# Query bias as rows in four column groups, two shared chunks two and one tiles earlier, identity products at tile 3

## The chip, the cores and the metric

The kernel runs on one core of one Trainium2 chip. The metric is the device time of one execution in microseconds (us), median over several runs; a profiled execution is one run more, with a trace of every instruction.

## The reference, cut to what matters

The program is one adaptive-LayerNorm block over X of 2 x 1024 tokens of 512 features. Six modulation vectors for each of the two batches come from `silu(c) @ wmod`. The first half is an attention of a special kind, the second a mixture of experts:

```python
h = _layernorm(x) * (1 + ca) + sa
# attention: A is one vector of 512 for each batch
Xn = _layernorm(h, gamma, beta)
Q, K, V = split(Xn @ W_in + b_in)
K, V = rotary(K), rotary(V)
A = 0.5 * sum_over_tokens(K / |K| * V / |V|) + 0.5
Y = (A * Q) @ W_out + b_out + h
x = x + ga * Y
h = _layernorm(x) * (1 + cb) + sb
# experts: a shared one of width 704 and the best 2 of 8 of width 352
x = x + gb * (shared(h) + routed(h))
```

Since Xn is `normed * gamma + beta`, the query has the constant part `beta @ W_q + b_q`, a vector of 512: the query bias.

## The kernel before, in words

Tokens go in 16 tiles of 128 rows. TensorE (PE) does the large products in three fp32r passes, high times high, high times low, low times high (`product3`, L1560 to L1562); ScalarE writes the high part of an operand (`tokens_hi`, `tokens2_hi`) and VectorE subtracts it from the original for the low part (`tokens_lo`, `tokens2_lo`). Each engine has its own instruction list, written out by hand, and works it off in order; semaphores (`wait_ge`, `then_inc`) tie them. There is no planner.

First pass, 16 tiles: K products, the transposes of the next tile, V products (`kv_matmul`, `transposes`), and the rotated, weighted sums of the tile before (`weighted_sums`). Among them stand small steps through one PSUM bank, named in the list `MISC`; `SLOT_A` says behind which tile's K products, `SLOT_B` behind which tile's V products. Each waits (`misc_read`) until the one before it in `MISC` has been read, by ScalarE or, for those in `BY_VECTOR`, by VectorE. `mod` (tile 5) makes the modulation rows in four groups of 32 columns; `q0` to `q3` turn the query weights; `qbias` (tile 6) makes `beta @ W_q` as a column: four output columns, four products of one column for each.

Then W_q, scaled by A, is multiplied by W_out (`m_matmul`, `h_matmul`), 179 to 188 us, so that the second rows need one product for each tile.

Second rows, a loop over 16 tiles t, 188 to 277 us. TensorE: `y_matmul(t)`, 13 products of 512 columns; at t = 6, 10, 14 `logit_parts` for four finished tiles and a tile later `gate_logits`; `transposes2(t - 2)`; and at the tiles of `Y_CHUNKS` a chunk of the shared expert's gate and up products for tiles 0 to 3 (`shared_gate_up(0, (m,))`, 24 products of 512 columns). Chunk 0 waits for `t2_lo` of four tiles, which VectorE raises in `tokens2_lo`. VectorE, in iteration t: `second_rows(t)` with the statistics (L1183, L989 to L991), `residual_part(t + 1)` (L1173), `tokens2_lo(t - 2)` (L1202), for t < 2 two blocks of the second batch's matrix (L1147, L1152), `ffn_rows(t)` (L1195, L1197), and for chunks `s_lo_of` and `s_mul_of`. ScalarE: `tokens2_hi(t - 2)` (L796, L797), `x_normed(t + 2)`, and for chunks `s_silu_of` and a tile later `s_hi_of`. `y_matmul(t)` waits for `x2_ready` of tile t - 2, `transposes2(t - 2)` for `h2_ready` of that tile. SyncE (SP) stores rows and loads the next X tile once for each t.

Behind the loop come the rest of the shared expert, the routing and, from about 400 us, a loop over experts, all with TensorE without gaps.

The activation buffer of the shared expert is `gbuf[n % 3]`, three buffers that lie in `bc_s`, `bc_c` and `bc_ga`; `bc_s` is still read by `ffn_rows` for the first batch.

Of the kernel before, what the change touches and what calls it, by code (L numbers as in the profile page):

```python
# [51 lines left out]
EW = 2 * DC * H + NR * D  # L52


Y_CHUNKS = {8: 0, 10: 1, 12: 2, 14: 3}


MISC = ["sin_a", "cos_a", "s1", "c1", "sin_b", "cos_b", "q0", "q1", "q2", "q3", "mod", "qbias", "a0", "a1"]
BY_VECTOR = ("c1", "mod", "qbias", "a0", "a1")
SLOT_A = {1: ["s1"], 2: ["sin_b"], 3: ["q0"], 4: ["q2"]}  # L60
SLOT_B = {0: ["sin_a", "cos_a"], 1: ["c1"], 2: ["cos_b"], 3: ["q1"], 4: ["q3"], 5: ["mod"], 6: ["qbias"], 9: ["a0"]}


def build(nc, X, W_in, b_in, W_out, b_out, gamma, beta, gate_w, w_gate, w_up, w_down,
# [10 lines left out]
    with ctx:  # L75
# [171 lines left out]
        rawkv = [slots[:, 2 + i, :].rearrange("p (k n) -> p k n", k=DC) for i in range(2)]  # L247
        cos, sin = slots[:, 0, 0:S], slots[:, 0, S:2 * S]
        MOD_SLOT = (2, 3, 1, 0)

        bank = [ctx.enter_context(nc.psum_tensor(f"bank{i}", [P, GN], F32)) for i in range(8)]
        T_BANKS, K_BANKS, V_BANKS, W_BANK, MISC_BANK = (0, 1), (2, 4), (3, 5), 6, 7
# [385 lines left out]
        def _(act):  # L638
# [31 lines left out]
            def tokens_hi(t):  # L670

                act.wait_ge(t_mm, t + 1)
                if t == 2 * GT:
                    act.wait_ge(misc_mm, MISC.index("mod") + 1)
                nc.scalar.activation(tokens(t, 0), chunked(bank[T_BANKS[t % 2]][:, :]), ACT.Copy).then_inc(t_hi, 1)

            def k_row(t):
# [19 lines left out]
            def read_misc(name):  # L697

                n = MISC.index(name)
                src = bank[W_BANK if name == "cos_a" else MISC_BANK][:, :]  # L700
                act.wait_ge(misc_mm, n + 1)
                if name == "s1":
                    last = nc.scalar.activation(bc_s[:, 1, :], src, ACT.Copy)
                elif name[0] == "q":
                    last = nc.scalar.activation(wqT[:, int(name[1]), :], src, ACT.Copy)
                else:
                    half = slice(0, GT) if name[-1] == "a" else slice(GT, NB)
                    src = src.rearrange("p (t f) -> p t f", t=GT)
                    if name[0] == "s":
                        last = nc.scalar.activation(cs[:, half, 0, :], src, ACT.Copy, scale=2.0)  # L710
                    else:
                        last = nc.scalar.activation(cs[:, half, 1, :], src, ACT.Identity, bias=ones[:, 0:1], scale=-2.0)
                last.then_inc(misc_read, 1)
# [92 lines left out]
            def s_silu_of(g, m):  # L806
                n = NS * g + m
                r = SM[m]
                act.wait_ge(s_gu_mm, n + 1)
                if n == 0:  # L810
                    act.wait_ge(h2_ready, NB)
                if n >= 3:
                    act.wait_ge(s_lo, n - 2)
                nc.scalar.activation(gbuf[n % 3][0:r, :], bank[gate_banks(g, m)[0]][0:r, :], ACT.Silu).then_inc(s_silu, 1)

            def s_hi_of(g, m):
                n = NS * g + m
                r = SM[m]
                act.wait_ge(s_mul, n + 1)
                if g:  # L820
                    act.wait_ge(s_down_mm, GT * g)
                nc.scalar.activation(gtS[0:r, m, 0, :], gbuf[n % 3][0:r, :], ACT.Copy).then_inc(s_hi, 1)

            for i in range(DC):
                m_block_hi(0, i)
# [136 lines left out]
        def _(dve):  # L962
# [242 lines left out]
            def s_mul_of(g, m):  # L1205
                n = NS * g + m
                r = SM[m]
                dve.wait_ge(s_silu, n + 1)
                up = bank[gate_banks(g, m)[0]][r:P, :] if r == P // 2 else bank[gate_banks(g, m)[1]][0:r, :]
                dve.tensor_tensor(gbuf[n % 3][0:r, :], gbuf[n % 3][0:r, :], up, ALU.mult)\  # L1210
                    .then_inc(s_mul, 1)

            def s_lo_of(g, m):
                n = NS * g + m
                r = SM[m]
                dve.wait_ge(s_hi, n + 1)
                to = gtS[:, m, 1, :] if r == P else gtS[r:P, m, 0, :]
                dve.tensor_tensor(to, gbuf[n % 3][0:r, :], gtS[0:r, m, 0, :].bitcast(F32), ALU.subtract)\
                    .then_inc(s_lo, 1)

            dve.wait_ge(ga_in, 16)
# [335 lines left out]
        def _(pe):  # L1557
# [62 lines left out]
            def misc(name):  # L1620

                n = MISC.index(name)
                to = bank[W_BANK if name == "cos_a" else MISC_BANK]
                if n < 2:
                    pe.wait_ge(bias_ready, 2)
                else:
                    pe.wait_ge(misc_read, n)
                if name in ("s1", "c1"):
                    last = spread_row((MISC_BANK), 1, 0 if name == "s1" else 1)
                elif name[0:3] in ("sin", "cos"):  # L1630
                    src = cos if name[0] == "s" else sin
                    pe.wait_ge(sincos if name[0] == "s" else sinsq, 1)
                    for j in range(GT):
                        at = (j + (GT if name[-1] == "b" else 0)) * P
                        last = nc.tensor.transpose(to[:, j * P:(j + 1) * P], src[:, at:at + P], ident[:, :])
                elif name == "qbias":
                    for m in range(DC):
                        for k in range(DC):
                            last = nc.tensor.matmul(to[:, m:m + 1], q_columns(k, m), gb_col[:, 1, k:k + 1],
                                                    start=k == 0, stop=k == DC - 1)  # L1640
                elif name[0] == "q":
                    pe.wait_ge(wq_in, 32)
                    for k in range(DC):
                        last = nc.tensor.transpose(to[:, k * P:(k + 1) * P], q_columns(k, int(name[1])), ident[:, :])
                elif name == "mod":
                    for k in range(DC):
                        pe.wait_ge(mod_in[k], 16)
                    for k in range(DC):
                        for v in range(4):
                            last = nc.tensor.matmul(to[Q4 * v:Q4 * v + B, :], scT[:, k, :],  # L1650
                                                    slots[:, MOD_SLOT[k], v * D:(v + 1) * D],
                                                    start=k == 0, stop=k == DC - 1)
                else:
                    b = int(name[1])
                    pe.wait_ge(arow_ready, b + 1)
                    pe.wait_ge(consts, 5)
                    for two in range(2):
                        nc.tensor.matmul(to[:, 0:2], arow[:, b, two:ROT:2], asel[:, 2 * two:2 * two + 2],
                                         start=two == 0, stop=two == 1)
                    for half in range(2):  # L1660
                        last = nc.tensor.matmul(to[:, 2 + half:3 + half], arow[:, b, half * P:(half + 1) * P],
                                                asel[:, 4:5], start=True, stop=True)
                last.then_inc(misc_mm, 1)

            def q_columns(k, m):

                return rawq[:, k, m:ROT:2] if m < 2 else rawq[:, k, m * P:(m + 1) * P]
# [68 lines left out]
            def shared_gate_up(g, chunks=range(NS)):  # L1736
                for m in chunks:
                    n, r = NS * g + m, SM[m]
                    if m == 0:
                        pe.wait_ge(t2_lo, GT * (g + 1))  # L1740
                        if g == 0:
                            pe.wait_ge(sg_lo, DC)
                    if n in range(1, DC + 1) or n == DC + 1:
                        pe.wait_ge(s_mul, n - (n == DC + 1))
                    elif n:
                        pe.wait_ge(s_mul, n - 1)
# [102 lines left out]
            def y_matmul(t):  # L1849
# [9 lines left out]
                if t == 0:  # L1859
                    pe.wait_ge(bh_ready, 1)  # L1860
                nc.tensor.matmul(to, pair1[:, b:b + 1].to_broadcast([P, P]), bh[:, :], start=False, stop=True)\
                    .then_inc(y_mm, 1)

            def transposes2(t):
                pe.wait_ge(h2_ready, t + 1)
                if t >= 2:
                    pe.wait_ge(t2_lo, t - 1)
                for k in range(DC):
                    last = nc.tensor.transpose(bank[T2_BANKS[t % 2]][:, k * P:(k + 1) * P],  # L1869
                                               hx[:, t % GT, k * P:(k + 1) * P], ident[:, :])  # L1870
                last.then_inc(t2_mm, 1)
# [16 lines left out]
                nc.tensor.transpose(bank[LG_BANK][:, g * P:(g + 1) * P], turned, ident[:, :]).then_inc(lg_mm, 1)  # L1888

            for t in range(NT):  # L1890
                y_matmul(t)
                if t >= 6 and t % GT == 2:
                    logit_parts((t - 6) // GT)
                if t >= 7 and t % GT == 3:
                    gate_logits((t - 7) // GT)
                if t >= 2:
                    transposes2(t - 2)
                if t in Y_CHUNKS:
                    shared_gate_up(0, (Y_CHUNKS[t],))
# [70 lines left out]
```

## Time and profile before

| | us |
|---|---|
| median of 3 runs | 719.1 |
| lowest and highest | 715.85, 719.9 |
| the profiled execution | 717.99 |
| its span, first to last instruction | 716.2 |
| TensorE products busy | 682.1 |
| VectorE, ScalarE, GpSimd busy | 469.6, 258.0, 169.4 |
| mean granted clock of TensorE | 0.982 of 2.4 GHz |

The span is shorter than the execution by what lies around it. Busy time of TensorE is that of its products, which overlap: a 512-column product lasts 0.39 us in the records and the next starts 0.23 us behind it, so starts, not durations, are what is subtracted here. A float32 product that isn't fp32r is two records. A clock of 0.50 is 1.2 GHz.

### The profile page before, as it was taken

How to read it: one execution, taken by the hardware profiler on the slowest of the kernel's cores; microseconds unless marked ns; L12 is line 12 of the kernel's file. 1: busy time of each engine (PE TensorE's matmuls, PEld its weight loads, DVE VectorE, ACT ScalarE, POOL GpSimd, SP SyncE). 2: the span in 40 equal slices, each digit the busy share in tenths (PEclk: the TensorE clock that was granted, in tenths of full speed). 3: DMA queues.
4: the chain of work that ended last, by engine and by line, in shares of the span. 5: the costliest groups of instructions: out<-in, count | busy, mean ns of one | idle time of the engine just before them, and what ended most of it. 6: DMA issues, size and time to landing. Idle time of an engine off the chain costs nothing.

```text
span 716.2 us, 10569 instructions
## 1 busy us (share of the span) xinstructions
PE 682.1 (95%) x3796; PEld 562.6 (79%) x3796; DVE 469.6 (66%) x967; ACT 258.0 (36%) x478; POOL 169.4 (24%) x221
## 2 busy tenths in 40 slices
PE   5899999999979999999999999999999999999992
PEld 1477677777857887887887887989898998989891
DVE  1987769836899886467767835665574847556451
ACT  1555344535344342412013024435362534436130
POOL 1232223310012110000000032334435353540403
PEclk9799999999999999999999999999999999999997
DMA  8923131104135624230320533657665575852505
GB/s 275 361 84 104 38 83 30 41 4 162 59 133 177 213 89 135 86 106 13 103 96 1 165 107 118 192 120 191 103 198 73 187 131 148 193 97 59 67 0 67
DMA packets 44219, 82.52 MB, mean 115 GB/s; under 512 B 7529, under 2 KB 15721, under 8 KB 43634
## 3 DMA queue, kind: packets, MB, share of 16 engines
q1 hardware_dynamic: 35730, 62.06, 26.8%
q0 software_dynamic: 8448, 19.93, 14.6%
q8 instruction: 24, 0.39, 0.2%
q14 instruction: 17, 0.14, 0.1%
HBM read 59.93 MB, written 23.22 MB: 116 GB/s over the span
## 4 chain that ended last, share of the span: by engine, by line
PE 63%; DVE 8%; issue 2%; ACT 1%; POOL 1%; POOLq 0%; DVEq 0%
PE bank L1560 19%; PE bank L1562 19%; PE bank L1561 19%; PE bank L1811 2%; PE bank L1791 1%; DVE rows L1183 1%; DVE u L1173 1%; DVE m L1147 1%; DVE st L989 1%; DVE hx L1195 1%; DVE mw L1152 1%; POOL out_rows L613 1%; PE bank L1869 1%; PE bank L1770 0%; PE bank L1882 0%
## 5 line engine op out<-in xcount | busy, mean ns | idle before, releaser
L1560 PE MATMUL bank<-ht,ew 128*128 128x288 f32 (+1 forms) x384 | 114.6, 299 | 0.2 <-DVE ht L1458 0.2
L1561 PE MATMUL bank<-ht,ew 128*128 128x288 f32 (+1 forms) x384 | 113.1, 294 | 0.0
L1562 PE MATMUL bank<-ht,ew 128*128 128x288 f32 (+1 forms) x384 | 112.8, 294 | 0.0
L613 POOL DMA_INDIRECT out_rows<-y,si x40 | 61.9, 1547 | 110.7 <-DVE y L1489 100.0
L1560 PE MATMUL bank<-xt,sgu 128*128 128x512 f32 x176 | 69.5, 395 | 0.4 <-DVE rows L1183 0.4
L1560 PEld LDWEIGHTS bank<-ht,ew 128*128 128x128 f32 (+1 forms) x384 | 68.7, 179 | 1.3 <-issue 0.6
L1561 PEld LDWEIGHTS bank<-ht,ew 128*128 128x128 f32 (+1 forms) x384 | 69.0, 180 | 0.3
L1562 PEld LDWEIGHTS bank<-ht,ew 128*128 128x128 f32 (+1 forms) x384 | 68.7, 179 | 0.0
L1561 PE MATMUL bank<-xt,sgu 128*128 128x512 f32 x176 | 68.7, 390 | 0.0
L1562 PE MATMUL bank<-xt,sgu 128*128 128x512 f32 x176 | 68.6, 390 | 0.0
L1560 PE MATMUL bank<-wkv,xt 128*128 128x512 f32 x128 | 55.2, 431 | 2.8 <-DVE xt L1018 2.8
L1448 DVE TENSOR_TENSOR ew<-ewst,ew 128x1408 fp32r<-128x1408 f32 (+2 forms) x32 | 40.5, 1289 | 18.9 <-ACT ew L872 11.3
L1562 PE MATMUL bank<-wkv,xt 128*128 128x512 f32 x128 | 52.0, 406 | 0.0
L1561 PE MATMUL bank<-wkv,xt 128*128 128x512 f32 x128 | 51.8, 404 | 0.0
L1489 DVE TENSOR_TENSOR y<-bank,gsel 128x512 f32<-128x512 f32 (+1 forms) x40 | 27.5, 688 | 35.2 <-PE bank L1562 35.2
L602 POOL DMA_INDIRECT picked<-h_d,gi x40 | 44.3, 1107 | 24.1 <-issue 9.8
L1560 PE MATMUL bank<-ew,gtR 128*128 128x512 f32 (+3 forms) x120 | 48.4, 403 | 0.0
L1561 PE MATMUL bank<-ew,gtR 128*128 128x512 f32 (+3 forms) x120 | 47.4, 395 | 0.0
L1562 PE MATMUL bank<-ew,gtR 128*128 128x512 f32 (+3 forms) x120 | 47.3, 394 | 0.0
L594 POOL COPY gi<-gidx 128x5 int32 (+1 forms) x8 | 1.9, 240 | 164.8 <-DVEq L1437 127.1
L544 POOL TENSOR_TENSOR rs<-ve,nhalf 128x1 f32<-128x1 f32 x16 | 15.4, 960 | 101.7 <-DVE ve L991 101.7
L1560 PEld LDWEIGHTS bank<-xt,sgu 128*128 128x128 f32 x176 | 33.1, 188 | 7.4 <-issue 0.8
(302 smaller groups left out, 1512.1 us busy)
## 6 DMA issues: line engine op xcount, KB each, us to landing
xring<-in_L_attn_X SPq DMA_DIRECT2D x32, 256.0 KB, 2.8
ewst<-in_L_ffn_w_gate SPq DMA_DIRECT2D x8, 704.0 KB, 5.3
ewst<-in_L_ffn_w_up SPq DMA_DIRECT2D x8, 704.0 KB, 4.3
slots<-in_L_wmod SPq DMA_DIRECT2D x4, 1024.0 KB, 6.1
x_d<-rows SPq DMA_DIRECT2D x16, 256.0 KB, 2.0
h_d<-hx SPq DMA_DIRECT2D x16, 256.0 KB, 2.0
xrow<-x_d SPq DMA_DIRECT2D x16, 256.0 KB, 2.8
out_rows<-xrow SPq DMA_DIRECT2D x16, 256.0 KB, 2.2
```

The source lines that it names most:

```text
L544: pool.tensor_tensor(rs[:, 2, t:t + 1], ve[:, 2, t:t + 1], nhalf[:, 0:1], ALU.pow).then_inc(rs3_ready, 1)
L602: pool.indirect_dma_start(out=picked[par][:, j, :], out_offset=None, in_=h2_d, in_offset=bass.IndirectOffsetOnAxis(ap=gi[:, par, j:j + 1], ...
L613: pool.indirect_dma_start(out=out, out_offset=bass.IndirectOffsetOnAxis(ap=si[0:CR[j], par, j:j + 1], axis=0), in_=y[0:CR[j], j, :], in_of ...
L989: link(dve.bn_stats(st6[:, :], row))
L1147: dve.scalar_tensor_tensor(m32[:, i, :], bank[M_BANKS[b][i]][:, :], gb_col[:, 0, i:i + 1], bc_ga[:, b, :], ALU.mult, ALU.mult).then_inc(m3 ...
L1152: dve.tensor_tensor(mw[:, b, 1, i, :], m32[:, i, :], mw[:, b, 0, i, :].bitcast(F32), ALU.subtract)\
L1448: last = dve.tensor_tensor(ew[par][0:r, 1, a:z], ewst[0:r, slot, at:at + z - a], ew[par][0:r, 0, a:z].bitcast(F32), ALU.subtract)
L1489: dve.tensor_tensor(y[0:r, j, :], bank[DOWN_BANKS[(par + j) % 2]][0:r, :], gsel[0:r, j, :], ALU.mult)\
L1560: nc.tensor.matmul(dst, a[0], b[0], start=first, stop=False)
L1561: nc.tensor.matmul(dst, a[0], b[1], start=False, stop=False)
L1562: return nc.tensor.matmul(dst, a[1], b[0], start=False, stop=last)
L1811: last = nc.tensor.transpose(bank[RT_BANKS[(par + s) % 2]][:, i * P:(i + 1) * P], picked[par][:, j, k * P:(k + 1) * P], ident[:, :])
```

## The change

1. A new small step `qrow` behind the K products of tile 6: four float32 products of 512 columns, one for each block of 128 input features, each into its own group of 32 output columns. ScalarE copies the result to a free slot, and `qbias` behind the V products of the same tile becomes four one-column products that add the four groups and turn the row. ScalarE's high part of tile 8 waits for `qbias` instead of `mod`, because it overwrites that slot.
2. `Y_CHUNKS`: chunk 0 stands behind tile 6 instead of 8, chunk 1 behind 9 instead of 10. The three buffers are taken in another order, so that the first chunk needs none that tiles below 8 still read; the waits of ScalarE follow.
3. `busy`: eight float32 products of a 128 x 128 identity with itself ahead of `y_matmul(3)` and eight behind it, whose result nobody reads.

```diff
-Y_CHUNKS = {8: 0, 10: 1, 12: 2, 14: 3}
+Y_CHUNKS = {6: 0, 9: 1, 12: 2, 14: 3}
-MISC = [..., "q3", "mod", "qbias", "a0", "a1"]
+MISC = [..., "q3", "mod", "qrow", "qbias", "a0", "a1"]
-SLOT_A = {1: ["s1"], 2: ["sin_b"], 3: ["q0"], 4: ["q2"]}
+SLOT_A = {1: ["s1"], 2: ["sin_b"], 3: ["q0"], 4: ["q2"], 6: ["qrow"]}
+        qrow = slots[:, 3, 0:D]
...
                 if t == 2 * GT:
-                    act.wait_ge(misc_mm, MISC.index("mod") + 1)
+                    act.wait_ge(misc_mm, MISC.index("qbias") + 1)
...
+                elif name == "qrow":
+                    last = nc.scalar.activation(qrow, src, ACT.Copy)
...
                 if n == 0:
+                    act.wait_ge(m32_ready, B * DC)
+                if n == 1:
                     act.wait_ge(h2_ready, NB)
...
-                nc.scalar.activation(gbuf[n % 3][0:r, :], ...Silu).then_inc(s_silu, 1)
+                nc.scalar.activation(gbuf[(n + 2) % 3][0:r, :], ...Silu).then_inc(s_silu, 1)
...
                 act.wait_ge(s_mul, n + 1)
+                if n == 0:
+                    act.wait_ge(y_mm, NB)
...
                 elif name == "qbias":
                     for m in range(DC):
-                        for k in range(DC):
-                            last = nc.tensor.matmul(to[:, m:m + 1], q_columns(k, m), gb_col[:, 1, k:k + 1],
-                                                    start=k == 0, stop=k == DC - 1)
+                        columns = qrow[:, m:ROT:2] if m < 2 else qrow[:, m * P:(m + 1) * P]
+                        last = nc.tensor.matmul(to[:, m:m + 1], columns, rowsel[:, 0:1], start=True, stop=True)
+                elif name == "qrow":
+                    pe.wait_ge(wq_in, 32)
+                    for k in range(DC):
+                        last = nc.tensor.matmul(quarter(to, k), gb_col[:, 1, k:k + 1].to_broadcast([P, Q4]), rawq[:, k, :],
+                                                start=True, stop=True)
...
                         if g == 0:
                             pe.wait_ge(sg_lo, DC)
+                            pe.wait_ge(m32_ready, B * DC)
...
+            def busy(to, times):
+                for _ in range(times):
+                    nc.tensor.matmul(to[:, 0:P], ident[:, :], ident[:, :], start=True, stop=True)
...
             for t in range(NT):
+                if t == 3:
+                    busy(bank[T2_BANKS[1]], 8)
                 y_matmul(t)
+                if t == 3:
+                    busy(bank[T2_BANKS[1]], 8)
```

VectorE's two operations on the chunks (`s_mul_of`, `s_lo_of`) take the buffers in the new order too.

## Rows read from the trace of the kernel before

**Rows 1.** The page: TensorE's busy time, and the clock in forty slices.

```profile
PE 682.1 (95%) x3796; PEld 562.6 (79%) x3796; DVE 469.6 (66%) x967; ACT 258.0 (36%) x478; POOL 169.4 (24%) x221
...
PEclk9799999999999999999999999999999999999997
```

**Rows 2.** The waits of TensorE: for whom, us in total, times, longest.

```profile
PE bank L1560 <- DVE rows L1183: 2.8, 3, 1.2
```

**Rows 3.** Order of time, TensorE, tiles 5 to 7: start, us, instruction.

```profile
77.45 0.40 PE L1617 MATMUL bank<-bv,pairs 128*128 128x512 f32 x1
77.78 3.62 PE L1650 MATMUL bank<-slots,scT 128*2 128x512 f32 x32
81.22 0.39 PE L1678 MATMUL bank<-prod,wtok 128*32 128x256 f32 x2
...
81.76 0.50 PE L1560 MATMUL bank<-wkv,xt 128*128 128x512 f32 x1
...
84.62 0.40 PE L1617 MATMUL bank<-bk,pairs 128*128 128x512 f32 x1
...
85.22 0.48 PE L1560 MATMUL bank<-wkv,xt 128*128 128x512 f32 x1
...
88.29 3.72 PE L1639 MATMUL bank<-gb_col,rawq 128*128 128x1 f32 x32
91.94 0.41 PE L1678 MATMUL bank<-prod,wtok 128*32 128x256 f32 x2
...
92.51 0.50 PE L1560 MATMUL bank<-wkv,xt 128*128 128x512 f32 x1
...
96.96 0.40 PE L1617 MATMUL bank<-bk,pairs 128*128 128x512 f32 x1
```

**Rows 4.** Stretches: length, PE, PEld, DVE, ACT, POOL busy, PE clock, DMA.

```profile
93.50:96.90 3.40, 3.40 (x9) 2.65 (x9) 1.26 (x5) 0.00 (x0) 0.74 (x2) 0.50 0.29 101
...
206.20:209.60 3.40, 3.40 (x9) 2.64 (x10) 3.30 (x7) 2.67 (x5) 0.99 (x1) 0.50 0.48 157
209.60:228.20 18.60, 17.59 (x110) 13.14 (x109) 18.05 (x34) 7.42 (x13) 3.95 (x4) 1.00 0.49 170
228.30:283.00 54.70, 54.31 (x309) 44.16 (x307) 43.45 (x79) 17.93 (x32) 8.44 (x9) 1.00 0.41 138
```

**Rows 5.** Order of time, TensorE, second rows; idle time before in brackets.

```profile
197.75 0.66 PE L1869 MATMUL bank<-ident,hx 128*128 128x128 f32 x4
199.61 0.51 PE L1560 MATMUL bank<-mw,xt 128*128 128x512 f32 x1 [1.21 <-DVE rows L1183]
...
204.17 0.66 PE L1869 MATMUL bank<-ident,hx 128*128 128x128 f32 x4 [1.28 <-DVE hx L1197]
206.03 0.69 PE L1560 MATMUL bank<-mw,xt 128*128 128x512 f32 x1 [1.21 <-DVE rows L1183]
...
218.22 1.08 PE L1882 MATMUL bank<-tmp,gw 128*32 128x128 f32 x32
219.24 0.66 PE L1869 MATMUL bank<-ident,hx 128*128 128x128 f32 x4
219.65 0.48 PE L1560 MATMUL bank<-mw,xt 128*128 128x512 f32 x1
...
222.72 0.27 PE L1888 MATMUL bank<-ident,lg 128*128 128x128 f32 x1
...
228.28 0.48 PE L1560 MATMUL bank<-xt,sgu 128*128 128x512 f32 x1
```

**Rows 6.** Order of time, VectorE and ScalarE.

```profile
81.47 0.69 DVE L1078 COPY mrow<-bank 128x512 f32<-128x512 f32 x1 [1.77 <-PE bank L1650]
...
214.23 0.74 DVE L1183 SCALAR_TENSOR_TENSOR rows<-u,mv,bank 128x512 f32<-128x512 f32 x1
...
221.18 0.68 DVE L1202 TENSOR_TENSOR xt<-bank,xt 128x512 fp32r<-128x512 f32 x1
...
207.09 0.60 ACT L796 ACTIVATE tmp<-bank 128x512 f32<-128x512 f32 x1
```

More of the change, by code:

```diff
@@ L52 @@
 EW = 2 * DC * H + NR * D
-Y_CHUNKS = {8: 0, 10: 1, 12: 2, 14: 3}
-MISC = ["sin_a", "cos_a", "s1", "c1", "sin_b", "cos_b", "q0", "q1", "q2", "q3", "mod", "qbias", "a0", "a1"]
+Y_CHUNKS = {6: 0, 9: 1, 12: 2, 14: 3}
+MISC = ["sin_a", "cos_a", "s1", "c1", "sin_b", "cos_b", "q0", "q1", "q2", "q3", "mod", "qrow", "qbias", "a0", "a1"]
 BY_VECTOR = ("c1", "mod", "qbias", "a0", "a1")
-SLOT_A = {1: ["s1"], 2: ["sin_b"], 3: ["q0"], 4: ["q2"]}
+SLOT_A = {1: ["s1"], 2: ["sin_b"], 3: ["q0"], 4: ["q2"], 6: ["qrow"]}
 SLOT_B = {0: ["sin_a", "cos_a"], 1: ["c1"], 2: ["cos_b"], 3: ["q1"], 4: ["q3"], 5: ["mod"], 6: ["qbias"], 9: ["a0"]}
@@ L813, in s_silu_of @@
                     act.wait_ge(s_lo, n - 2)
-                nc.scalar.activation(gbuf[n % 3][0:r, :], bank[gate_banks(g, m)[0]][0:r, :], ACT.Silu).then_inc(s_silu, 1)
+                nc.scalar.activation(gbuf[(n + 2) % 3][0:r, :], bank[gate_banks(g, m)[0]][0:r, :], ACT.Silu).then_inc(s_silu, 1)
             def s_hi_of(g, m):
@@ L819, in s_hi_of @@
                 act.wait_ge(s_mul, n + 1)
+                if n == 0:
+                    act.wait_ge(y_mm, NB)
                 if g:
                     act.wait_ge(s_down_mm, GT * g)
-                nc.scalar.activation(gtS[0:r, m, 0, :], gbuf[n % 3][0:r, :], ACT.Copy).then_inc(s_hi, 1)
+                nc.scalar.activation(gtS[0:r, m, 0, :], gbuf[(n + 2) % 3][0:r, :], ACT.Copy).then_inc(s_hi, 1)
             for i in range(DC):
@@ L1209, in s_mul_of @@
                 up = bank[gate_banks(g, m)[0]][r:P, :] if r == P // 2 else bank[gate_banks(g, m)[1]][0:r, :]
-                dve.tensor_tensor(gbuf[n % 3][0:r, :], gbuf[n % 3][0:r, :], up, ALU.mult)\
+                dve.tensor_tensor(gbuf[(n + 2) % 3][0:r, :], gbuf[(n + 2) % 3][0:r, :], up, ALU.mult)\
                     .then_inc(s_mul, 1)
@@ L1217, in s_lo_of @@
                 to = gtS[:, m, 1, :] if r == P else gtS[r:P, m, 0, :]
-                dve.tensor_tensor(to, gbuf[n % 3][0:r, :], gtS[0:r, m, 0, :].bitcast(F32), ALU.subtract)\
+                dve.tensor_tensor(to, gbuf[(n + 2) % 3][0:r, :], gtS[0:r, m, 0, :].bitcast(F32), ALU.subtract)\
                     .then_inc(s_lo, 1)
```

## The prediction, made before the changed kernel ran

> **What bounds the kernel now.** I read four views in turn. The page's first two parts come first: the products of TensorE are busy for 682.1 us of the 716.2 us span, and its strip of forty slices shows full tenths nearly everywhere, so time is won only by fewer or shorter products, by closing a gap between them, or by keeping the granted clock at its upper level [rows 1]. The strip of the clock has no full slice of low clock behind the start, but it averages over 18 us. The second view is the list of waits: TensorE's longest sum behind the start-up is 2.8 us, three waits for the rows that VectorE writes in `second_rows` [rows 2]. The third is the order of time, read in the two places that the change touches: tile 6 of the first pass [rows 3] and tiles 2 to 9 of the second rows [rows 5]. The fourth is the table by stretches, which names the clock inside them [rows 4].
>
> At tile 6 TensorE has no gap. The 16 one-column products of `qbias` (32 passes, since float32 goes through twice) start at 88.29, and the sums behind them at 91.94: 3.65 us, 0.114 us a pass. The K products of tile 7 start at 92.51 and their bias product at 96.96, 4.45 us, while the same stretch of tile 6 took 81.76 to 84.62, 2.86 us [rows 3]. The table says why: from 93.5 to 96.9 the granted clock is 0.50, that is 1.2 instead of 2.4 GHz [rows 4]. So the low clock costs 4.45 - 2.86 = 1.59 us here. What TensorE did before it fell was 3.65 us of one-column products.
>
> In the second rows the bound is VectorE up to tile 8. It is busy 18.05 of 18.60 us between 209.6 and 228.2 [rows 4], one tile each 4.5 us, while a tile of TensorE takes 3.07 us (219.65 to 222.72, tile 7) and 0.4 us of transposes (219.24 to 219.65) [rows 5]. TensorE idles 1.21, 1.28 and 1.21 us at 199.61, 204.17 and 206.03, and then runs at clock 0.50 from 206.2 to 209.6 [rows 4, 5]. From 228.28, when chunk 0 starts, it is TensorE that bounds: busy 54.31 of 54.70 us [rows 4]. Hence a delay before 228.28 counts only as far as it moves the point from which TensorE runs without gaps.
>
> **The query bias.** Removed: 3.65 us of TensorE. Added: `qrow`, four float32 products of 512 columns side by side in four column groups, and four one-column products instead of 16. The nearest row for the first is `mod`, 16 such products in four groups, 77.78 to 81.22, so 3.44 / 4 = 0.86 us for a round of four [rows 3]. Changing into column groups shows as a start 0.33 us behind the bias product at 77.45, where 0.23 us is the usual step, so 0.10 us [rows 3]. The second part is 8 passes x 0.114 = 0.91 us. Sum 0.86 + 0.10 + 0.91 = 1.87 us, gain 3.65 - 1.87 = 1.8 us. Bounds: with 0.3 us for two changes of form and the first read of a new tile the gain is 1.5 us; without any it is 1.9 us.
>
> The Trainium skill, "TensorEngine Tiling (Array Packing)", section Key Properties, says that a change of tiling mode drains the TensorE, which speaks against splitting the step in two forms. The trace agrees that there is a price and has it at 0.10 us a change [rows 3]; no run here shows a larger one, and the sum stands on the row.
>
> New waits of this part. `qrow` on TensorE waits for the reading of `mod`, which VectorE does at 81.47, against a start of `qrow` at about 85.2, where tile 6's V products begin now [rows 3, 6]: 3 us of cover. Queued behind it are the V products of tile 6. `qbias` waits for ScalarE's copy of `qrow`, 0.6 us as any of its passes over 512 columns [rows 6], while TensorE does the V products, 3.07 us from 85.22 to 88.29 [rows 3]: covered. ScalarE then waits at the high part of tile 8 for `qbias` in place of `mod`; the transposes that it needs stand behind `qbias` on TensorE anyway, so nothing. No DMA is moved.
>
> The clock. After the change the one-column work is 0.91 us between dense products, a quarter of what stood before the fall. I count the 1.59 us as gained. Bounds: 0 (the clock falls nevertheless) and 1.7 us (half of the 3.4 us stretch).
>
> **The identity products at tile 3.** 16 products, 32 passes x 0.114 = 3.6 us, in two groups of 1.8 us. The first starts when the transposes end, about 198.2, and ends about 200.0, where tile 3 starts now at 199.61 after its wait: 0.4 us late. The second group follows tile 3 and ends about 205.0; the transposes of tile 1 then come at 205.0 instead of 204.17, still ahead of ScalarE, which reads them at 207.09 [rows 5, 6]. Tile 4 starts at 206.03 as before, since it waits for rows of VectorE, probably at full clock, and so ends about 1.4 us earlier. That brings nothing: VectorE takes tile 4 at 214.23 without having waited [rows 6], and tile 5 of TensorE waits for VectorE. So 0 us, both ways; cover 3 us. If VectorE had that time free, the part would give up to 1.4 us; if the cover were gone, it would cost at most its 0.8 us of delay.
>
> **Chunk 0 from tile 8 to tile 6, chunk 1 from 10 to 9.** The products, 24 of 0.23 us a chunk, are the same. Chunk 0 needs the low parts of tiles 0 to 3, and VectorE writes that of tile 3 in its iteration 5, at 221.18, done at 221.86 [rows 6]. TensorE reaches the new place when the transposes of tile 4 are issued, at 219.65 [rows 5]. So it waits 221.95 - 219.65 = 2.3 us, and behind it are queued tile 7 and the transposes of tile 5, which would have run. From then on it has no gap: tiles 7 and 8 now find their rows ready. Before, between 219.65 and 228.28 it did two tiles (2 x 3.07), two sets of transposes (2 x 0.4) and one small transpose (0.1), 7.0 us of work in 8.63 us: 1.6 us lost [rows 5]. New loss 2.3, old loss 1.6: +0.7 us. VectorE waits for tile 7 then about 2 us, but what it makes next, the rows of tile 7, is needed two tiles later, behind 3.5 us each of TensorE: covered. Chunk 1 one tile earlier finds TensorE busy on both sides: 0. The rotated buffers and the waits for `m32_ready` and `y_mm` are long met: 0.
>
> What the clock does after the 2.3 us is not in the trace. The rows on both sides: after gaps of 1.28 and 1.21 us with only transposes between, 3.1 us without dense products, it fell for 3.4 us; after the single gap of 1.21 us at 199.61 it did not [rows 4, 5]. Here 3.7 us pass between the last product of tile 6 and chunk 0 (218.22 to 221.95), of which 1.0 us are the logit parts and 0.4 us transposes. I take it as nearer to the first: the clock falls for 3.4 us, and since TensorE is the bound from there, half of it counts, +1.6 us (a little may fall in the wait). Bounds 0 and 3.4 us (two such stretches).
>
> **The sum.** -1.8 - 1.6 + 0 + 0.7 + 1.6 = -1.1 us. The profiled execution took 717.99 us (span 716.2 and 1.8 us around it); the median of the runs is 719.1 us, and they go from 715.85 to 719.9. I set the base between the two at 718.5 us, so the forecast is 717.4 us.
>
> **Rivals.** (a) The clock holds through the wait at chunk 0, because the logit parts and transposes keep TensorE awake. For it: 3.44 us of narrow `mod` products did not lower it, as the next K products took their usual 2.86 us [rows 3]. Against it: the fall at 206.2. It gives -2.7 us, 715.8 us. (b) Slower than before: the low clock behind the new wait lasts two stretches, costing 3.4 us: -1.8 - 1.6 + 0.7 + 3.4 = +0.7 us, 719.2 us. It decides from a clock cost of 2.7 us. Against it: both falls in these rows lasted one stretch. (c) The fall at 93.5 is not from the one-column products and stays: -1.8 + 0.7 + 1.6 = +0.5 us, 719.0 us. For it: it came 1.6 us after they had ended. (d) The chunk doesn't wait, the change doing just what its place suggests, filling the 1.6 us of gaps: -1.8 - 1.6 - 1.6 = -5.0 us, 713.5 us. Against it: the order of VectorE's work puts the low part of tile 3 at 221.18.
>
> **How the numbers follow.** Forecast 0.45, (a) 0.25, (b) 0.12, (c) 0.10, (d) 0.08. Medians of runs that spread over 4 us add about 1.2 us to each. A half per cent, 3.6 us, is about what a measurement of this kernel can tell from no change. Faster than that, under 715.5 us, takes (d), nearly half of (a) and a little of the forecast and of the spread: 0.26. Slower, over 722.7 us, takes the tails of (b) and (c) and things unseen: 0.04. The rest, 0.70, is within. The range runs from 1 us under (a) to 1 us over (b): 714.8 to 720.2 us.
>
> **What would show it.** In the new profile: `qrow` of about 0.9 us before tile 6's V products and `qbias` of 0.9 us behind them; clock 1.00 through the K products of tile 7; tile 4 of the second rows at full clock but VectorE's rows of tile 5 no earlier; a wait of about 2.3 us ahead of chunk 0, put down to the low parts of `xt` by VectorE, and a low clock behind it. The prediction is wrong if chunk 0 starts without that wait, if the clock falls elsewhere, or if VectorE idles between tiles 2 and 6.

## The result and the profile after

The changed kernel took 715.31 us in the median (714.2 to 715.62, four executions) against 719.14 us before: ratio 0.9953, 95% interval 0.9931 to 0.9975. Its span is 713.6 us where it was 716.2. The forecast was 717.4 us, and the time is nearer to rival (a), 715.8 us. It is 3.8 us under the median of before; between the two profiled executions, 717.99 and 715.50 us, it is 2.5 us. The kernel before scatters by more than the difference between the two measures: 35 later executions of it ran from 715.68 to 720.73 us with a median of 718.18. The ratio is not the quotient of the two medians; 0.9953 stands for 3.4 us, with 1.8 to 5.0 us as its interval.

Order of time of TensorE after the change, the stretch of [rows 3]; `product3` is now L1567 to L1569, the columns are start, us, instruction:

```profile
76.61 0.40 PE L1624 MATMUL bank<-bv,pairs 128*128 128x512 f32 x1
76.94 3.62 PE L1661 MATMUL bank<-slots,scT 128*2 128x512 f32 x32
...
83.78 0.40 PE L1624 MATMUL bank<-bk,pairs 128*128 128x512 f32 x1
84.02 0.60 PE L1606 MATMUL bank<-ident,hz 128*128 128x128 f32 x4
84.54 1.06 PE L1650 MATMUL bank<-rawq,gb_col 128*32 128x512 f32 x8
85.54 0.50 PE L1567 MATMUL bank<-wkv,xt 128*128 128x512 f32 x1
...
88.64 0.97 PE L1646 MATMUL bank<-rowsel,slots 128*128 128x1 f32 x8
89.54 0.41 PE L1689 MATMUL bank<-prod,wtok 128*32 128x256 f32 x2
...
90.10 0.50 PE L1567 MATMUL bank<-wkv,xt 128*128 128x512 f32 x1
...
92.97 0.39 PE L1624 MATMUL bank<-bk,pairs 128*128 128x512 f32 x1
```

In the kernel before, the V products of tile 6 start 85.22 - 84.86 = 0.36 us behind the transposes' start:

```profile
84.86 0.60 PE L1599 MATMUL bank<-ident,hz 128*128 128x128 f32 x4
```

`qrow` makes that 85.54 - 84.02 = 1.52 us, so it costs 1.16 us; `qbias` costs 89.54 - 88.64 = 0.90 us; the V products between take 3.10 instead of 3.07 us. Together 2.09 us in place of 3.65 us [rows 3]: 1.56 us of work gained. The K products of tile 7 take 92.97 - 90.10 = 2.87 us, where they took 4.45: 1.58 us of low clock are gone.

The second rows of the changed kernel, to be held against [rows 5]; in brackets the idle time before and what ended it:

```profile
193.75 0.66 PE L1886 MATMUL bank<-ident,hx 128*128 128x128 f32 x4
194.24 1.95 PE L1879 MATMUL bank<-ident 128*128 128x128 f32 x16
195.94 0.48 PE L1567 MATMUL bank<-mw,xt 128*128 128x512 f32 x1
...
199.03 1.95 PE L1879 MATMUL bank<-ident 128*128 128x128 f32 x16
200.81 0.60 PE L1886 MATMUL bank<-ident,hx 128*128 128x128 f32 x4
202.02 0.50 PE L1567 MATMUL bank<-mw,xt 128*128 128x512 f32 x1 [0.61 <-DVE rows L1190]
...
214.22 1.08 PE L1899 MATMUL bank<-tmp,gw 128*32 128x128 f32 x32
215.23 0.66 PE L1886 MATMUL bank<-ident,hx 128*128 128x128 f32 x4
217.91 0.50 PE L1567 MATMUL bank<-xt,sgu 128*128 128x512 f32 x1 [2.03 <-DVE xt L1209]
```

and its stretches (length; busy time and instructions of PE, PEld, DVE, ACT, POOL; granted clock; DMA share and GB/s), to be held against [rows 4]:

```profile
89.50:93.00 3.50, 3.50 (x22) 2.56 (x23) 3.36 (x8) 0.69 (x2) 1.34 (x2) 1.00 0.89 232
202.00:205.60 3.60, 3.27 (x13) 2.37 (x13) 3.49 (x7) 2.87 (x6) 0.99 (x1) 1.00 0.48 148
205.60:217.90 12.30, 9.44 (x70) 6.80 (x70) 11.92 (x24) 5.63 (x10) 2.96 (x3) 1.00 0.55 189
217.90:224.00 6.10, 6.09 (x27) 4.99 (x27) 5.73 (x10) 0.27 (x1) 0.99 (x1) 1.00 0.40 135
224.00:279.60 55.60, 55.21 (x315) 44.95 (x314) 44.10 (x79) 19.44 (x35) 8.45 (x9) 1.00 0.39 136
```

The identity products stand where they were expected; tile 4 runs at full clock; VectorE stays full (11.92 of 12.30 us). TensorE stands idle for 2.03 us ahead of chunk 0, until VectorE has written the low part of tile 3. And behind that wait the clock is 1.00: the fall that the forecast counted did not come.

**Where the 2.6 us of span lie.** A table of distances serves from here on. Each is taken between starts of the same product in both traces: the K bias products of the first pass at tiles 5 and 7, the y bias products of the second rows at tiles 0 and 15, the first rank product of the routing (`both` by `upper`, L1914 in the kernel before), the last product of all.

| distance, us | before | changed | changed, 2nd profile |
|---|---|---|---|
| start of the span to K of tile 5 | 74.02 | 73.17 | 73.05 |
| K of tile 5 to K of tile 7 | 22.94 | 19.80 | 19.80 |
| K of tile 7 to y of tile 0 | 94.35 | 94.34 | 94.34 |
| y of tile 0 to y of tile 15 | 84.76 | 85.44 | 85.40 |
| y of tile 15 to the rank product | 43.76 | 44.07 | 45.30 |
| the rank product to the last | 382.90 | 382.97 | 382.92 |

The bias gives 3.14 us and the second rows take 0.68 us. The rest that differs lies in places that no part of the change touches: the start (0.85 us less), the stretch behind the second rows (0.31 us more) and the end behind the last product (13.85 us for 13.49).

### The profile page after: what moved, and what is told of

It is laid out like the page before. It is cut to its first block, busy times and chain, and to the rows that moved or that the text cites. A ratio compares the mean times of both kernels' runs of the same rounds, so it can differ in the third digit from the quotient of the medians.

```text
span 713.6 us, 10605 instructions
## 1 busy us (share of the span) xinstructions
PE 681.0 (95%) x3812; PEld 561.0 (79%) x3812; DVE 469.7 (66%) x967; ACT 258.5 (36%) x479; POOL 170.5 (24%) x221
## 4 chain that ended last, share of the span: by engine, by line
PE 62%; DVE 8%; issue 2%; DMA 1%; ACT 1%; POOL 1%; SPq 0%; POOLq 0%; DVEq 0%
PE bank L1567 19%; PE bank L1569 19%; PE bank L1568 19%; PE bank L1823 2%; DMA sdraw<-in_L_ffn_sw_down 1%; PE bank L1803 1%; DVE m L1154 1%; DVE rows L1190 1%; DVE st L996 1%; DVE u L1180 1%; DVE mw L1159 1%; POOL out_rows L614 1%; DVE hx L1202 1%; PE bank L1886 1%; PE bank L1782 0%
## 5 line engine op out<-in xcount | busy, mean ns | idle before, releaser
L1567 PE MATMUL bank<-ht,ew 128*128 128x288 f32 (+1 forms) x384 | 114.6, 298 | 0.2 <-DVE ht L1465 0.2
L1569 PE MATMUL bank<-ht,ew 128*128 128x288 f32 (+1 forms) x384 | 112.8, 294 | 0.0
L1567 PE MATMUL bank<-xt,sgu 128*128 128x512 f32 x176 | 69.6, 395 | 2.6 <-DVE xt L1209 2.0
L1567 PEld LDWEIGHTS bank<-ht,ew 128*128 128x128 f32 (+1 forms) x384 | 68.7, 179 | 1.3 <-issue 0.7
L1569 PEld LDWEIGHTS bank<-ht,ew 128*128 128x128 f32 (+1 forms) x384 | 68.7, 179 | 0.0
L1569 PE MATMUL bank<-xt,sgu 128*128 128x512 f32 x176 | 68.7, 390 | 0.0
L1567 PE MATMUL bank<-wkv,xt 128*128 128x512 f32 x128 | 54.5, 425 | 2.6 <-DVE xt L1025 2.6
L1569 PE MATMUL bank<-wkv,xt 128*128 128x512 f32 x128 | 50.9, 398 | 0.0
L1568 PE MATMUL bank<-wkv,xt 128*128 128x512 f32 x128 | 50.8, 397 | 0.0
L1567 PE MATMUL bank<-ew,gtR 128*128 128x512 f32 (+3 forms) x120 | 48.4, 403 | 0.0
L1569 PE MATMUL bank<-ew,gtR 128*128 128x512 f32 (+3 forms) x120 | 47.3, 394 | 0.0
L1567 PEld LDWEIGHTS bank<-xt,sgu 128*128 128x128 f32 x176 | 33.1, 188 | 10.0 <-DVE xt L1209 2.3
```

The source lines that it names most:

```text
L1567: nc.tensor.matmul(dst, a[0], b[0], start=first, stop=False)
L1568: nc.tensor.matmul(dst, a[0], b[1], start=False, stop=False)
L1569: return nc.tensor.matmul(dst, a[1], b[0], start=False, stop=last)
```

## The experiments

Ratios are against executions of the kernel before on the same chip, taken along with those of the variant, with a 95% interval. There are three such groups, each on a chip of its own, with 35, 23 and 11 executions of before and medians of 718.18, 718.01 and 717.71 us. As above, a ratio is not the quotient of two medians; where both are given and differ, the ratio with its interval is the firmer one.

### The query bias alone

The kernel before with the three pieces of `qrow` and the new `qbias`, chunks and tile 3 untouched.

```diff
-SLOT_A = {1: ["s1"], 2: ["sin_b"], 3: ["q0"], 4: ["q2"]}
+SLOT_A = {1: ["s1"], 2: ["sin_b"], 3: ["q0"], 4: ["q2"], 6: ["qrow"]}
```

> Only the query bias in rows. Theory (work and clock both count): TensorE's work falls by 1.6 us (qrow 1.16 and qbias 0.90 and 0.03 us of other spacing, against 3.65 us) and the low clock that stood at 93.5 to 96.9 is gone, 1.6 us: 3.1 us less than before, ratio 0.9956, about all of what the change gave. Rival (the clock falls there anyway, or the time is absorbed by VectorE or the loads in the second rows): 1.6 us or less, ratio 0.998 or above.

Measured: 714.34 us (713.5 to 717.33, 12 executions), ratio 0.9958 (0.9943 to 0.9973): 3.8 us less by the medians, 3.0 us (1.9 to 4.1) by the ratio. K of tile 5 to K of tile 7 is 19.80 us and the second rows are 84.78 us as before. So the bias is the whole gain, and the 1.56 + 1.58 = 3.1 us of the traces account for it within the interval. Tile 4 of the second rows ran at low clock here, as before the change.

### The same one-column products in two pieces

All 16 products stay, half of them ahead of the V products of tile 6 and half behind.

```diff
+                if t == 6:
+                    pe.wait_ge(misc_read, MISC.index("qbias"))
+                    for m in range(2):
+                        for k in range(DC):
+                            nc.tensor.matmul(bank[MISC_BANK][:, m:m + 1], q_columns(k, m), gb_col[:, 1, k:k + 1],
+                                             start=k == 0, stop=k == DC - 1)
                 kv_matmul(t, 1)
...
-                    for m in range(DC):
+                    for m in range(2, DC):
```

> The same 16 one-column products of the query bias as before, but half of them ahead of the V products of tile 6 and half behind: the work is the same 3.65 us in two pieces of 1.8 us. Theory (one long piece of one-column work lowers the clock): clock 1.00 from 88 to 100, 1.6 us less than before, ratio 0.9978. Rival (the fall has another cause): a stretch of clock 0.50 remains near 93 and the time stays, ratio 1.000.

Measured: 715.48 us (714.45 to 718.31, 12 executions), ratio 0.9969 (0.9955 to 0.9984): 2.7 us less by the medians, 2.2 us (1.1 to 3.2) by the ratio, with not one product fewer. The second piece and the clock are visible in the profile (order of time, then two stretches):

```profile
82.66 0.40 PE L1617 MATMUL bank<-bk,pairs 128*128 128x512 f32 x1
...
88.20 1.84 PE L1639 MATMUL bank<-gb_col,rawq 128*128 128x1 f32 x16
...
93.42 0.39 PE L1617 MATMUL bank<-bk,pairs 128*128 128x512 f32 x1
```

```profile
84.00:86.00 2.00, 2.00 (x15) 1.87 (x16) 1.90 (x6) 0.76 (x3) 0.13 (x1) 1.00 0.38 85
86.00:93.80 7.80, 7.80 (x50) 6.36 (x49) 5.61 (x14) 1.50 (x3) 3.21 (x7) 1.00 0.61 181
```

K of tile 5 to K of tile 7 is 21.36 us, that is 22.94 - 1.58. One profile alone would not prove it, since two of the six profiles with the products in one piece show 21.36 us too: the identity products alone, and the first of the chunks alone (below). Of the other four, three have 22.91 to 22.95 us, where the low clock lasted 3.4 us, and one has 24.47 us, where it lasted 6.8. So the clock costs 0, 1.6 or 3.1 us from one execution to the next, 1.3 us in the mean of the six. The ratio over twelve executions is what shows that the split helps; that it helps by more than 1.6 us is not shown, since its interval reaches down to 1.1 us. The three values of the distance also part the two halves of the gain without any scatter: 21.36 - 19.80 = 1.56 us is the work, and 22.94 - 21.36 = 1.58 us the clock.

### The identity products alone

```diff
+                if t == 3:
+                    busy(bank[T2_BANKS[1]], 8)
                 y_matmul(t)
+                if t == 3:
+                    busy(bank[T2_BANKS[1]], 8)
```

> Only the identity products at tile 3. Theory (VectorE is the bound of tiles 1 to 8): tile 4 runs at full clock, VectorE's rows come at the same distances of 4.5 us, TensorE reaches chunk 0 at the same time; no change, ratio 0.999 to 1.001. Rival (the identity products keep the clock up in later tiles in executions where it would fall nearer to chunk 0): 1 to 1.7 us faster in the median, ratio 0.998 or below, and a narrower spread.

Measured: 719.51 us (715.23 to 722.36, 12 executions), ratio 1.0019 (1.0000 to 1.0039), a little above the expected 0.999 to 1.001. The second rows take 84.77 us in its profile, against 84.76 before: nothing gained or lost there, although tile 4 itself is done 1.6 us earlier (y of tile 0 to y of tile 4 takes 17.57 us for 19.17). Even that can't be put down to the identity products by this profile: the bias in two pieces has 17.57 us without them. What its profile has more, 2.3 us, lies behind the rank product (385.20 us from there to the last product, 382.90 before); most of it are waits of TensorE for the one-hot rows of VectorE, 2.3 us in five waits where the others have 1.0 us in two (view of waits: us in total, times, longest):

```profile
PE bank L1770 <- DVE hot_col L1273: 2.3, 5, 0.5
```

That is far from tile 3 and in no other of the profiles. Whether the identity products have any part in it is asked of pairs of kernels.

### Pairs with and without the identity products

The changed kernel once more, and the changed kernel without its identity products:

> The changed kernel once more, for its median over more executions and a second profile. The four executions so far gave 715.3 us. Theory A (the parts add: bias -3.8, identity +1.3, chunks +1.5 us, each as measured alone): 717.2 us, ratio 0.9985. Theory B (the identity products and the chunks cost nothing together, only the 0.7 us of the longer wait): 715.1 us, ratio 0.9956.

> The changed kernel without the identity products at tile 3. If they are free, as the trace says (TensorE reaches the tile 6 of the second rows at the same time with and without them): the same as the changed kernel to 0.1 per cent. If they keep the clock up for chunk 0: 1 us or more slower than the changed kernel. If they cost what they seemed to cost alone (+1.3 us): 1.3 us faster.

Measured: 715.79 us (713.34 to 716.54, nine executions), ratio 0.9958 (0.9942 to 0.9973) with them; 715.53 us (713.77 to 717.11, nine), ratio 0.9959 (0.9940 to 0.9978) without. So the parts do not add as measured alone, which would have given a ratio of 0.9985 by the medians, and the second profile of the changed kernel repeats the first (table above), clock 1.00 behind the wait included. The profile without them has y of tile 0 to y of tile 15 at 85.41 us.

The bias and the identity products, with the chunks back at 8 and 10:

```diff
-Y_CHUNKS = {6: 0, 9: 1, 12: 2, 14: 3}
+Y_CHUNKS = {8: 0, 10: 1, 12: 2, 14: 3}
```

> The bias in rows and the identity products, chunks behind the tiles 8, 10, 12 and 14 as before (the buffers in the new order). If the identity products are free: the time of the bias alone, ratio 0.9958. If they cost what they seemed to cost when alone: ratio 0.9975 or above. If they help: 0.994 or below.

Measured: 713.89 us (713.45 to 715.2, six executions), ratio 0.9951 (0.9939 to 0.9964), beside 0.9958 for the bias alone. This is the changed kernel without the moved chunks, and the gain is all there. Three pairs (this one, the one above, and the one at tile 7 below: 0.9937 with, 0.9931 without) agree: the identity products make no difference that can be measured. Only the pair above (0.9958 and 0.9959) was measured within one group of runs, and the 0.2 per cent that the products seemed to cost alone is not explained.

### The chunks alone

The kernel before with `Y_CHUNKS = {6: 0, 9: 1, 12: 2, 14: 3}`, the new order of buffers and the waits that belong to it.

> Only chunk 0 at tile 6, chunk 1 at tile 9 and the buffers. Theory (chunk 0 waits 2.0 us for the low part of tile 3): 0.7 us slower than before with the clock up, ratio 1.001; where the clock falls behind the wait 2.3 us slower, 1.0032. Rival (filling VectorE's idle time later gives it back, or the clock is kept better): the same or faster, ratio below 1.000.

Measured: 719.7 us, ratio 1.0024 (1.0000 to 1.0048), and the twelve times lie in two bunches: five from 715.64 to 717.75 us with a mean clock of 0.985 to 0.989, seven from 719.12 to 723.05 us with 0.977 to 0.982. Two further profiled executions show where the clock falls.

> The chunks alone once more, for a second profile. In the first call the executions of it with a mean clock of 0.985 and more took 715.6 to 717.8 us, those with 0.982 and less 719.1 to 723.1 us, and the profiled one was of the first bunch, with no low clock between 31 and 706 us. Theory: an execution of the upper bunch shows the low clock behind the query bias (costing 1.6 us) and behind the wait of chunk 0 (about 1.7 us). Rival: the low clock of the upper bunch lies elsewhere, in the start or ahead of VectorE's bound, and its time comes from another wait.

> The same kernel a third time, since one look falls in either bunch; the same expectations.

They took 722.25 and 718.55 us, the first profile 716.87 us. In the second profile, order of time and three stretches:

```profile
87.72 4.61 PE L1643 MATMUL bank<-gb_col,rawq 128*128 128x1 f32 x32
...
222.85 0.50 PE L1564 MATMUL bank<-xt,sgu 128*128 128x512 f32 x1 [2.03 <-DVE xt L1206]
```

```profile
90.20:97.00 6.80, 6.80 (x29) 5.21 (x29) 2.96 (x8) 0.37 (x2) 1.63 (x4) 0.51 0.47 147
206.90:209.90 3.00, 2.94 (x7) 2.37 (x8) 2.90 (x7) 2.90 (x6) 0.98 (x1) 0.52 0.60 171
223.60:226.90 3.30, 3.30 (x9) 2.53 (x9) 3.20 (x7) 0.00 (x0) 0.78 (x1) 0.50 0.49 179
```

and in the first profile, the stretches that answer to them:

```profile
86.10:93.50 7.40, 7.40 (x55) 6.42 (x54) 5.70 (x14) 1.50 (x3) 2.46 (x6) 1.00 0.64 198
205.00:208.00 3.00, 2.42 (x12) 1.55 (x11) 2.89 (x5) 1.30 (x3) 0.00 (x0) 1.00 0.39 141
218.50:223.00 4.50, 4.50 (x20) 3.70 (x21) 4.36 (x9) 0.00 (x0) 0.99 (x1) 1.00 0.44 168
```

| distance, us | 1st profile | 2nd profile | 3rd profile |
|---|---|---|---|
| K of tile 5 to K of tile 7 | 21.36 | 24.47 | 22.95 |
| y of tile 0 to y of tile 15 | 85.44 | 86.97 | 87.03 |
| execution | 716.87 | 722.25 | 718.55 |

The same kernel, the same 2.03 us of wait in all three; the clock fell at the bias not at all, for 6.8 us and for 3.4 us, costing 0, 3.1 and 1.6 us, and behind the wait not at all and twice for 3.4 us, costing 0, 1.5 and 1.6 us. In the second profile it fell while the one-column products still ran (from 90.3, the products from 87.72 to 92.33). So the price that the forecast named for the wait is real and right in size, 1.6 us, and it is paid in some executions and not in others. Low clock at tile 4 (206.9) costs nothing: the second and third profile have it, and chunk 0 still starts 30.6 us behind y of tile 0 in all three.

### The wait filled

The chunks alone, and between the transposes of tile 4 and chunk 0 nine identity products into an idle bank, so that TensorE does not idle there.

```diff
+                if t == 6:
+                    pe.wait_ge(m32_ready, B * DC)
+                    for _ in range(9):
+                        nc.tensor.matmul(bank[UP_BANKS[1]][:, 0:P], ident[:, :], ident[:, :], start=True, stop=True)
                 if t in Y_CHUNKS:
```

> Only the chunks moved, as in the run of the chunks alone, and the 2.0 us wait ahead of chunk 0 filled with nine float32 identity products of 128 columns (about 1.9 us), whose result nobody reads. The chunks alone gave two bunches of times, 715.6 to 717.8 and 719.1 to 723.1 us. Theory (the upper bunch is a fall of the clock behind the wait): the upper bunch is gone or rarer, median 717.0 to 718.5 us. Rival (the upper bunch has another cause, or the products don't count for the clock): median as for the chunks alone, 719.7 us.

Measured: 719.02 us (717.58 to 719.77, 12 executions), ratio 1.0007 (0.9996 to 1.0019). Nothing lies above 719.8 us, where the unfilled kernel had six of twelve. But the median is above the expected 717.0 to 718.5 us, the intervals of the two kernels overlap, and the mean of the granted clocks is no higher (0.982 against 0.983). The two were also measured on different chips, and on that of the unfilled one the identity products alone, with no chunk moved, had five of twelve above 719.8 us. So that the filling took the upper times away is likely and not shown. In its profile the products take the place of the wait and chunk 0 runs at clock 1.00:

```profile
218.68 2.17 PE L1906 MATMUL bank<-ident 128*128 128x128 f32 x18
220.88 0.50 PE L1564 MATMUL bank<-xt,sgu 128*128 128x512 f32 x1
```

```profile
220.90:226.40 5.50, 5.50 (x24) 4.58 (x25) 5.33 (x10) 0.00 (x0) 0.98 (x1) 1.00 0.44 162
```

One profile of the unfilled kernel had clock 1.00 there too. What stays is the delay: y of tile 0 to y of tile 15 is 85.50 us, 0.7 us over before.

### Chunk 0 behind tile 7, where it need not wait

The changed kernel without the identity products, and with them, chunk 0 one tile later.

```diff
-Y_CHUNKS = {6: 0, 9: 1, 12: 2, 14: 3}
+Y_CHUNKS = {7: 0, 9: 1, 12: 2, 14: 3}
```

> The bias in rows, chunk 0 behind tile 7 instead of 6, chunk 1 behind 9, no identity products. Theory: TensorE no longer waits for the low part of tile 3, and loses only about 0.5 us between the tiles 6 and 7 instead of 1.6 us (before) or 2.3 us (changed): 1.1 us less than the bias alone, 713.2 us, ratio 0.993. Rival: another wait of VectorE takes the place of it (rows of tile 7 late) and the time is that of the bias alone, ratio 0.9958.

> The changed kernel with chunk 0 behind tile 7 instead of 6, all else as changed. Against the changed kernel: no wait for the low part of tile 3, 1.7 us less, 714.0 us, ratio 0.9935. Against the same kernel without identity products (713.0 us): the same if these are free, 1 us slower if they cost in themselves.

Measured: 713.01 us (712.13 to 714.63, six executions), ratio 0.9931 (0.9912 to 0.9950) without identity products; 713.48 us (712.03 to 713.92, six), ratio 0.9937 (0.9925 to 0.9950) with them. The second rows take 83.70 and 83.67 us, 1.1 us less than before and 1.7 us less than the changed kernel. The profile without identity products has ahead of chunk 0 only the wait that stood there before:

```profile
212.40 0.40 PE L1873 MATMUL bank<-bh,pair 128*128 128x512 f32 x1
...
217.87 0.66 PE L1881 MATMUL bank<-ident,hx 128*128 128x128 f32 x4 [0.37 <-DVE hx L1204]
218.28 0.48 PE L1567 MATMUL bank<-xt,sgu 128*128 128x512 f32 x1
```

Of all versions these two are the fastest; they beat the kernel before by 0.6 to 0.7 per cent. Against the changed kernel the traces give 1.7 us, the ratios 1.5 to 1.9 us with intervals that overlap a little, and the medians of the same group of runs 715.79 - 713.01 = 2.8 us.

## Why the prediction came out as it did

**The query bias.** The work was forecast at -1.8 us with bounds of -1.5 and -1.9, and is -1.56 us. The term that was mis-sized is the price of `qrow`: 1.16 us for 0.96. The round of 0.86 us was read off four rounds in a row; here one round alone takes 85.54 - 84.54 = 1.00 us, and the way into it 0.16 us in place of 0.10 (it starts 0.52 us behind the transposes, where the V products started 0.36 us behind them). What makes a lone round longer is not shown. The clock term, -1.6 us, is right for this pair of profiles (1.58 us) and within the interval of the two-piece experiment (1.1 to 3.2 us); that it is 0, 1.6 or 3.1 us by the execution was not foreseen. Rival (c) is out: the split alone gains, with an interval clear of no change, and none of the eight profiles with the new or the split bias has a fall between tile 5 and the second rows, where four of the six with the old one have it.

**The identity products.** Forecast 0, 0 in the trace (84.77 against 84.76 us), and no difference in three pairs. The cover was named rightly: VectorE takes tile 4 at 210.23, 22.92 us behind the y bias product of tile 0 at 187.31, and before it was 214.23 - 191.31 = 22.92 us too [rows 6]. With them tile 4 ran at full clock in all five profiles; without them it did in three of nine. So they probably do keep the clock up, at a place where TensorE is not the bound.

**The chunks.** The wait was forecast at 2.3 us, reckoned from the start that chunk 0 would have had behind the transposes; by the same measure it was 217.91 - (215.23 + 0.41) = 2.27 us, of which 2.03 are idle by the records. The net cost was forecast at +0.7 us and was +0.68. Rival (d) is out.

**The clock behind the wait.** This is the step that failed: "I take it as nearer to the first: the clock falls for 3.4 us [...] +1.6 us". In all three profiles of kernels that have both the new bias and chunk 0 at tile 6 (two of the changed kernel and one without identity products) it did not fall. It is not that the wait can't lower it: with the old bias it did in two profiles of three, at just the price forecast. So whether the clock falls behind a gap of this size is decided by something that differs from execution to execution, and the forecast put into its sum in full what comes and goes. Whether it is rarer with the new bias, and why, is not settled; in the six profiles at hand with chunk 0 at tile 6 and the wait unfilled, a fall behind the wait came only where one had come at the bias too, but six are few.

**The base.** I set it at 718.5 us; the larger samples of before have medians of 718.2, 718.0 and 717.7. The sum by measured terms: 718.2 - 1.56 - 1.58 + 0 + 0.68 + 0 = 715.7 us, for 715.3 and 715.8 measured. By rival (a)'s terms it was 715.8: what came is rival (a), to which I had given 0.25. My forecast was 2.1 us too high, 1.6 us of it by the clock term, and the time fell into the range only because the range was drawn around that rival too. Rival (b), two stretches behind the wait, was seen nowhere.

## What to carry to other kernels

Price a block of narrow products twice: for its own time and for the clock that the products behind it get; here the two were equal, 1.56 and 1.58 us, and merely cutting the block in two around full-width products won the second back. Before moving work forward into a gap, find which operand it needs and when that is written in the other engine's order: one tile later the same chunk gained 1.1 us, one tile too early it lost 0.7 us. Where a term comes and goes with the execution, one profile can't give its size: take the distances between equal instructions from several profiles, and let the ratio over many executions, with its interval, decide.

## What the runs showed of the hardware that was not expected

The one-column products lowered the clock without TensorE idling at all: it was busy for all of 88.3 to 91.9 and granted half clock from 93.5 [rows 3, 4]; of the six profiles with them in one piece, four had such a fall, which cost 1.6 us and once 3.1.

The start of the program scatters by nearly as much as the whole bias is worth: the K bias product of tile 5 came between 71.67 and 74.59 us. And the stretch from y of tile 15 to the rank product took 43.69 to 45.44 us in kernels that are alike there. In the profile of the bias alone, 44.98 us, TensorE's gap there traces back to ScalarE waiting for the shared expert's down weights to land:

```profile
ACT sd L649 <- DMA sdraw<-in_L_ffn_sw_down: 4.7, 1, 4.7
...
PE bank L1563 <- DVE bc_ga L1213: 1.1, 1, 1.1
```

All fourteen profiles say the same. The transfer is issued when the second rows are stored, 5.48 or 5.49 us behind y of tile 15 in each of them; ScalarE gets to use it between 13.05 and 14.82 us; and from there to the rank product it is 30.62 to 30.66 us in each. So the landing time is the scatter of this stretch, up to 1.7 us, more than half of what the bias gives. Loading the weights earlier was not tried.
